# One row-maximum instruction over two PSUM banks instead of two in the layer attention of a hybrid kernel

## The chip, the cores and the metric

The kernel runs on one core of a Trainium2 chip. Its time is the device time of one execution in microseconds; of several executions the median is given. TensorE is called PE here (its weight loads PEld), VectorE DVE, ScalarE ACT, GpSimd POOL, and SyncE, which issues every DMA of this stage, SP.

## What is computed

The program has a stack of four layers, then a feed-forward network with sixteen experts, a second attention, and the experts again. The change touches only the attention inside the four layers. Cut to it, the reference is:

```
# x: 16 sequences of 256 tokens, 128 features; H = 16 heads of 8 features
for l in range(4):
    m = mamba(x, ...)
    x = ln(x + m, g1[l], be1[l])
    qkv = einsum('bsd,od->bso', x, W_qkv[l]) + b_qkv[l]    # -> q, k, v per head
    scores = einsum('bhqd,bhkd->bhqk', q, k) / sqrt(8)
    wts = softmax(scores, axis=-1)                         # 16 x 16 x 256 x 256
    o = einsum('bhqk,bhkd->bhqd', wts, v)
    x = ln(x + o @ W_ao[l].T + b_ao[l], g2[l], be2[l])
    x = x + mlp(x)
```

The softmax takes off each row's maximum before the exponential, so a maximum over 256 keys is needed for each of 16 sequences, 16 heads and 256 queries, in each of four layers.

## The kernel before

**Two passes over the scores.** For each sequence (called a batch, `b`, 0 to 15) the scores are computed twice. The first pass (`row`, line 948) has the queries on the partitions: one head is two matmuls of 128 queries by 256 keys, which fill one PSUM bank of 512 columns. DVE reduces the bank to two maxima per partition (`maxima`, line 1849) into `hmx`. Heads alternate between banks 0 and 1 (`ps[:, o % 2, :]`, `o` is the place in `ORDER`). When all 16 heads of a batch are reduced, DVE makes the negated maxima in two parts (`minus_max`, lines 1857 and 1859), PE transposes them (line 982), ACT copies them to `hmt` (line 1438), and SP sends them by two DMAs (`send_max`, line 571) into two spare rows of the operand `hqk`. In the second pass (`score`, line 960) the keys are on the partitions and the two spare rows take off the maximum inside the matmul, so that ACT can take the exponential straight from PSUM (line 1445). `values` (line 973) multiplies by v.

**The steady loop.** Each batch has eight steps, p0 to p7. In step p PE computes the row scores of two heads of a later batch (heads 8 to 15 of the next batch in p0 to p3, heads 0 to 7 of the one after it in p4 to p7) and, side by side in other rows of its array, the scores of heads 2p and 2p+1 of the current batch. PE's matmuls of a step wait until both maxima of the step before are done:

```
pe.wait_ge(hd_exp, nth(hd_exp, B, p - 2))
if both:
    pe.wait_ge(hd_max, nth(hd_max, B + ahead, o - 1))
```

Beside the scores a step has one more piece of PE work: p0 the v projection (line 941), p2 the q and k projections of the batch three ahead (`project_qk`, lines 935 and 936), p4 the softmax sums (line 989), p7 the output projection (line 995), p1, p3, p5 and p6 `values`, p5 the transposes of the maxima too. DVE has the two maxima of each step, `minus_max` at the end of p3, and one addition in p7 (line 1865).

**What hangs on p2.** From the projections of p2 a chain runs on other engines: ACT adds the bias (line 1425), POOL splits q and k into parts (`hqks`: casts at lines 2136 and 2137, subtractions at lines 2140 and 2141), SP spills them to HBM with four DMAs (line 556), later brings them back in another layout with four more (`scatter`, line 565). SP's queue is in order; in each batch it holds the spill of batch b+3, then `send_max` of batch b+1, then the scatter of batch b+3. The matmuls of p0 of the next batch wait for `send_max` to land (`pe.wait_ge(hd_mx, ...)`).

**Before the loop.** A layer's attention starts with the row scores of batch 0 (16 heads) and of half of batch 1 (8 heads), 12 pairs of heads. Here each head waits only for its own bank: `pe.wait_ge(hd_max, nth(hd_max, l * BATCH + b, o - 2))` at line 953, so that PE fills one bank while DVE reduces the other. Then comes the first `send_max`, behind the third spill and scatter in SP's queue.

**After it.** Batches 13 to 15 have fewer of these parts (no projections and no spill from batch 13 on, no row scores from p4 of batch 14 on).

Of the kernel before, what the change touches and what calls it, by code (L numbers as in the profile page):

```python
# [14 lines left out]
ALU = mybir.AluOpType  # L15
ACT = mybir.ActivationFunctionType
AX = mybir.AxisListType
# [7 lines left out]
LAYERS, STATES, HEADS, DH = 4, 64, 16, 8  # L25
# [9 lines left out]
GROUPS = 4  # L35
# [23 lines left out]
def build_program(nc, x_d, mw_d, xp_d, tw_d, w12_d, gw_d, idx_d, out_d):  # L59
    ctx = ExitStack()  # L60
    with ctx:
# [7 lines left out]
        def at(name, shape, dt=F32, where=None):  # L69

            where = top if where is None else where
            n = 4
            for s in shape[1:]:
                n *= s
            t = nc.alloc_sbuf_tensor_at(name, shape, dt, offset=where[0])
            where[0] += (n + 63) // 64 * 64
            return t
# [129 lines left out]
        hmx = at("hmx", [P, 4, 2, HEADS], where=w)  # L207
# [27 lines left out]
        ps = ctx.enter_context(nc.psum_tensor("ps", [P, 8, CH], F32))  # L235
# [7 lines left out]
        def counter(name, n=1):  # L243

            s = sem(name)
            counted[s.name] = (s, n)
            return s
# [115 lines left out]
        hd_am = counter("hd_am", 16)  # L363
        hd_max = counter("hd_max", 16)
# [32 lines left out]
        def nth(s, c, k=0):  # L397

            n = counted[s.name][1]
            return n * c + (n * CREDIT + k + 1)  # L400

        def every(s, c):

            n = counted[s.name][1]
            return n * c + n * (CREDIT + 1)
# [24 lines left out]
        def scattered(e, third, r):  # L430

            return e * (NR[r] * SPREAD) + third * SPREAD + SPREAD
# [13 lines left out]
        def heads(eng, step, last):  # L446

            step(0, 0, first=True)
            with eng.Fori(0, 3) as i:
                for k in range(4):  # L450
                    step(i * 4 + (1 + k), (1 + k) % 4)
            step(13, 1, n3=False)
            step(14, 2, n2=False, n3=False)
            step(15, 3, n1=False, n2=False, n3=False)
            last()
# [8 lines left out]
        def _(sp):  # L464
# [28 lines left out]
            def attention(e, probsparse):  # L493
                def send_max(b, half, r):

                    B = e * BATCH + b

                    for row, part, ready in ((96, mh, at_mh), (97, ml, at_ml)):
                        sp.wait_ge(ready, nth(ready, B, half))
                        sp.dma_start(qv[r][row:row + 1, 8 * half:8 * half + 8, :].bitcast(F32),  # L500
                                     part[0:8, half, :].bitcast(F32)).then_inc(at_mx[half], 16)

                def spill_qk(b, third, r, first=False):

                    B = e * BATCH + b
                    if not first:
                        before, rb = third + (r + 2) // 3 - 1, (r + 2) % 3
                        sp.wait_ge(at_scat[rb], scattered(e, before, rb))
                    sp.wait_ge(at_lo, nth(at_lo, B, 1))
                    sp.dma_start(qk_d.rearrange("a p t n -> p a t n"), qks[:].bitcast(F32)).then_inc(at_spill, 16)  # L510

                def spread_qk(b, r):


                    B = e * BATCH + b
                    sp.wait_ge(at_spill, every(at_spill, B))
                    sp.wait_ge(at_sc, nth(at_sc, B - 3, 7))
# [1062 lines left out]
        def _(dve):  # L1580
            V = nc.vector
# [261 lines left out]

            def head_attention(l, part="middle"):
                def maxima(b, o, r):
                    B = l * BATCH + b
                    j, g = ORDER[o] // 4, ORDER[o] % 4
                    dve.wait_ge(hd_am, nth(hd_am, B, o))
                    V.tensor_reduce(hmx[:, r, :, 4 * g + j], ps[:, o % 2, :].rearrange("p (t k) -> p t k", t=2), AX.X,  # L1849
                                    ALU.max).then_inc(hd_max, 1)  # L1850

                def minus_max(b, r):

                    B = l * BATCH + b
                    dve.wait_ge(hd_max, nth(hd_max, B, 15))
                    dve.wait_ge(hd_tp, nth(hd_tp, B - 1))
                    V.tensor_scalar(hhl[:, :, 0, :], hmx[:, r], -1.0, None, ALU.mult).then_inc(hd_mhi, 1)
                    dve.wait_ge(hd_mhi, nth(hd_mhi, B))
                    V.scalar_tensor_tensor(hhl[:, :, 1, :], hmx[:, r], -1.0, hhl[:, :, 0, :].bitcast(F32),
                                           ALU.mult, ALU.subtract).then_inc(hd_mlo, 1)  # L1860

                def add_out(b):
                    B = l * BATCH + b
                    dve.wait_ge(hd_aop, nth(hd_aop, B))
                    V.scalar_tensor_tensor(xa[:, ds(b * SEQ, SEQ)], ps[:, 7, 0:SEQ], hbo[:],
                                           xa[:, ds(b * SEQ, SEQ)], ALU.add, ALU.add).then_inc(hd_ao, 1)

                def step(b, r, first=False, n1=True, n2=True, n3=True):
                    for p in range(8):
                        ahead, o, ra = (1, 8 + 2 * p, (r + 1) % 4) if p < 4 else (2, 2 * p - 8, (r + 2) % 4)  # L1870
                        if n1 if p < 4 else n2:
                            maxima(b + ahead, o, ra)
                            maxima(b + ahead, o + 1, ra)
                        if p == 3 and n1:
                            minus_max(b + 1, (r + 1) % 4)
                        if p == 7 and not first:
                            add_out(b - 1)

                if part == "end":
                    return [lambda: add_out(15)]  # L1880

                for o in range(HEADS):
                    maxima(0, o, 0)
                minus_max(0, 0)
                for o in range(8):
                    maxima(1, o, 1)
                heads(dve, step, lambda: None)

            def gates(n):
# [138 lines left out]
            with dve.Fori(0, LAYERS) as l:  # L2028
                dve.wait_ge(load_m, l * 48 + 48)
                dve.sem_inc(waited, 1)  # L2030
                m1(l)
                m2(l)
                m3(l)
                dve.wait_ge(load_f, l * 16 + 16)
                dve.sem_inc(waited, 1)
                dve.wait_ge(load_t, l * 16 + 16)
                dve.sem_inc(waited, 1)
                norm(l * 2 + 1, gain=("g1", "be1"), hooks={"apart": None})
                head_attention(l)
                end = head_attention(l, "end")  # L2040
                norm(l * 2 + 2, gain=("g2", "be2"),
                     hooks={(0, 2): end[0],
                            (1, 0): lambda: f_parts(l, 0), (1, 1): lambda: f_parts(l, 1)})
                f(l)
# [283 lines left out]
```

## Time and profile before

| what | value |
|---|---|
| median of 3 runs | 3271.56 us (3259.83 to 3273.29) |
| profiled execution, own time | 3267.46 us |
| its span, first to last instruction | 3265.8 us |
| mean granted clock of PE | 0.933 |
| busy: PE, DVE, ACT, POOL | 86%, 57%, 54%, 25% |
| maxima (line 1849) | 1024 instructions, 660.1 us busy |

The four layer attentions take about 275 us each of the span. Times in the rows are microseconds from the span's start. A busy share is a mean over stages with different limits, so it says little about one stage; the idle time in front of an instruction, with what ended it, says more.

### The profile page before, as it was taken

How to read it: one execution, taken by the hardware profiler on the slowest of the kernel's cores; microseconds unless marked ns; L12 is line 12 of the kernel's file. 1: busy time of each engine (PE TensorE's matmuls, PEld its weight loads, DVE VectorE, ACT ScalarE, POOL GpSimd, SP SyncE). 2: the span in 40 equal slices, each digit the busy share in tenths (PEclk: the TensorE clock that was granted, in tenths of full speed). 3: DMA queues.
4: the chain of work that ended last, by engine and by line, in shares of the span. 5: the costliest groups of instructions: out<-in, count | busy, mean ns of one | idle time of the engine just before them, and what ended most of it. 6: DMA issues, size and time to landing. Idle time of an engine off the chain costs nothing.

```text
span 3265.8 us, 56810 instructions
## 1 busy us (share of the span) xinstructions
PE 2812.3 (86%) x17396; PEld 1737.5 (53%) x17396; DVE 1863.4 (57%) x3116; ACT 1770.7 (54%) x2669; POOL 805.1 (25%) x864
## 2 busy tenths in 40 slices
PE   7877799787899787898788879999966999799999
PEld 4444446444455444464444446666644777466666
DVE  4567735577546577445677345444536887454444
ACT  6457656367655377654477654444422666544443
POOL 0212200122100222101122014444440000244444
PEclk8989999799899699999799989999987999899999
DMA  2134300244200344101344000000002332000000
GB/s 94 43 94 108 79 6 8 67 100 107 52 12 8 89 103 104 26 8 33 93 99 98 6 7 1 0 0 0 0 1 94 98 101 72 4 4 7 3 6 6
DMA packets 95850, 150.50 MB, mean 46 GB/s; under 512 B 13152, under 2 KB 81248, under 8 KB 89312
## 3 DMA queue, kind: packets, MB, share of 16 engines
q1 hardware_dynamic: 95712, 148.77, 17.3%
q8 instruction: 73, 1.20, 0.2%
q14 instruction: 65, 0.53, 0.1%
HBM read 79.00 MB, written 67.11 MB: 45 GB/s over the span
## 4 chain that ended last, share of the span: by engine, by line
PE 43%; issue 23%; DVE 13%; POOL 11%; DMA 4%; SPq 2%; ACT 2%; DVEq 1%; POOLq 1%; ACTq 0%
POOL hhlo L2179 9%; DVE hmx L1849 9%; PE ps L948 7%; PE ps L754 3%; PE ps L973 2%; PE ps L717 2%; PE ps L681 2%; PE ps L687 2%; PE ps L793 2%; PE ps L829 2%; PE ps L1154 1%; DMA hqk<-hqk_scratch 1%; PE ps L815 1%; SPq L556 1%; DMA hqk_scratch<-hqks 1%
## 5 line engine op out<-in xcount | busy, mean ns | idle before, releaser
L1849 DVE TENSOR_REDUCE hmx<-ps 128x2 f32<-128x512 f32 x1024 | 660.1, 687 | 310.9 <-PE ps L948 310.1
L1445 ACT ACTIVATE hpt<-ps 128x1024 f32<-128x1024 f32 x512 | 522.3, 1024 | 289.5 <-PE ps L960 287.7
L2179 POOL TENSOR_TENSOR hhlo<-hh,hhh 128x512 fp32r<-128x512 f32 x320 | 414.8, 1296 | 463.0 <-ACT hhh L1524 462.1
L948 PE MATMUL ps<-hqk 24*128 24x256 f32 x2048 | 309.0, 359 | 235.1 <-DVE hmx L1849 189.1
L948 PEld LDWEIGHTS ps<-hqk 24*128 24x128 f32 x2048 | 191.5, 206 | 461.8 <-DVE hmx L1849 412.1
L1519 ACT ACTIVATE sil<-ps 128x512 f32<-128x512 f32 x320 | 191.0, 597 | 441.4 <-PE ps L1156 437.4
L1943 DVE TENSOR_TENSOR su<-ps,sil 128x512 f32<-128x512 f32 x256 | 177.1, 692 | 326.7 <-PE ps L1156 318.4
L973 PE MATMUL ps<-hpt,hvx 128*32 128x256 f32 x4096 | 299.3, 413 | 1.9 <-ACT hpt L1445 1.6
L960 PE MATMUL ps<-hqk 26*128 26x256 f32 x2048 | 272.2, 348 | 1.7 <-ACT hpt L1445 1.2
L1524 ACT ACTIVATE hhh<-hh 128x512 fp32r<-128x512 f32 x320 | 199.5, 624 | 40.9 <-DVE hh L1946 26.8
L2136 POOL CAST hqks<-hqk 128x512 fp32r<-128x512 f32 x64 | 40.5, 633 | 673.3 <-ACT hqk L1425 641.8
L1946 DVE TENSOR_TENSOR hh<-ps,su 128x512 f32<-128x512 f32 x256 | 177.0, 691 | 8.7
L960 PEld LDWEIGHTS ps<-hqk 26*128 26x128 f32 x2048 | 162.7, 197 | 25.5 <-ACT hpt L1445 19.7
L1757 DVE TENSOR_REDUCE mxs<-ps 128x2 f32<-128x512 f32 x256 | 164.1, 680 | 12.9 <-PE ps L793 11.7
L1373 ACT ACTIVATE pt<-ps 128x1024 f32<-128x1024 f32 x128 | 130.3, 1019 | 66.1 <-PE ps L815 64.3
L973 PEld LDWEIGHTS ps<-hpt,hvx 128*32 128x32 f32 x4096 | 113.0, 115 | 94.0 <-issue 22.9
L1154 PE MATMUL ps<-xh,w2h 128*128 128x512 f32 x324 | 154.7, 477 | 0.0
L2148 POOL TENSOR_TENSOR hon<-hraw,hrec 128x512 f32<-128x512 f32 x64 | 81.6, 1275 | 270.4 <-ACT hrec L1459 270.4
L1350 ACT ACTIVATE hid<-ps,mw 128x512 f32<-128x512 f32 x128 | 83.1, 689 | 106.3 <-PE ps L746 105.2
L1154 PE MATMUL ps<-xh,w1h 128*128 128x512 f32 x324 | 128.2, 396 | 13.1 <-DVE hh L1940 9.6
L1167 PE MATMUL ps<-hhh,w3h 128*128 128x512 f32 x320 | 127.3, 398 | 4.4 <-POOL hhlo L2179 4.4
L1155 PE MATMUL ps<-xl,w1h 128*128 128x512 f32 x324 | 128.8, 397 | 0.0
(247 smaller groups left out, 5593.1 us busy)
## 6 DMA issues: line engine op xcount, KB each, us to landing
hqk_scratch<-hqks SPq DMA_DIRECT2D x256, 192.0 KB, 3.1
hqk<-hqk_scratch SPq DMA_DIRECT2D x256, 192.0 KB
qk_scratch<-qks SPq DMA_DIRECT2D x16, 768.0 KB, 3.3
k<-qk_scratch SPq DMA_DIRECT2D x16, 384.0 KB
qv<-qk_scratch SPq DMA_DIRECT2D x64, 96.0 KB
mw<-mw_in SPq DMA_DIRECT2D x10, 516.5 KB, 3.9
w12raw<-w_in SPq DMA_DIRECT2D x1, 2560.0 KB, 9.5
streams<-x_in SPq DMA_DIRECT2D x8, 256.0 KB, 4.8
```

What stands on the lines that cost most here:

```text
L948: return mm(ps[:, o % 2, qt * SEQ:(qt + 1) * SEQ], hqk[r][32 * g:32 * g + 24, 0, j, qt * P:(qt + 1) * P], hqk[r][32 * g:32 * g + 24, 1, j, ...
L960: return mm(ps[:, 2 + g, kt * SEQ:(kt + 1) * SEQ], hqk[r][32 * g:32 * g + 26, 1, j, kt * P:(kt + 1) * P], hqk[r][32 * g:32 * g + 26, 0, j, ...
L973: last = mm(ps[32 * g:32 * g + 32, 6, (j // 2) * SEQ:(j // 2 + 1) * SEQ], hvx[r][:, kt, g, j, :], hpt[:, j, g, kt, :], start=j % 2 + kt == ...
L1154: mm(o, wh[:, k, :], xh[:, u, :], start=True, stop=False)
L1445: A(hpt[:, j, g:g + 2, :, :], ps[:, 2 + g:4 + g, :], ACT.Exp, scale=QSCALE).then_inc(hd_exp, 1)
L1519: A(sil[:, k % 2, :], ps[:, k % 2, :], ACT.Silu).then_inc(e_s, 1)
L1524: A(hhh[:, b % 4, :], hh[:, b % 2, :], ACT.Copy).then_inc(e_hi, 1)
L1757: V.tensor_reduce(mxs[:, r, h, :], ps[:, h % 2, :].rearrange("p (t k) -> p t k", t=2), AX.X, ALU.max)\
L1849: V.tensor_reduce(hmx[:, r, :, 4 * g + j], ps[:, o % 2, :].rearrange("p (t k) -> p t k", t=2), AX.X, ALU.max).then_inc(hd_max, 1)
L1943: V.tensor_tensor(su[:, s, :], ps[:, 2 + s, :], sil[:, s, :], ALU.mult).then_inc(e_t, 1)
L1946: V.tensor_tensor(hh[:, s, :], ps[:, 4 + s, :], su[:, s, :], ALU.mult).then_inc(e_m, 1)
L2179: G_.tensor_tensor(hhlo[:, k % 4, :], hh[:, k % 2, :], hhh[:, k % 4, :].bitcast(F32), ALU.subtract).then_inc(e_lo, 1)
```

## The change

In the layer attention one instruction now reduces both banks, two heads at a time, where there were two instructions of one bank each. Its output is four maxima per partition, for two heads and two halves of the queries; it waits for the row scores of both heads and then counts `hd_max` up by two. The diff:

```
             def head_attention(l, part="middle"):
                 def maxima(b, o, r):
+
                     B = l * BATCH + b
                     j, g = ORDER[o] // 4, ORDER[o] % 4
-                    dve.wait_ge(hd_am, nth(hd_am, B, o))
-                    V.tensor_reduce(hmx[:, r, :, 4 * g + j], ps[:, o % 2, :].rearrange("p (t k) -> p t k", t=2), AX.X,
-                                    ALU.max).then_inc(hd_max, 1)
+                    dve.wait_ge(hd_am, nth(hd_am, B, o + 1))
+                    V.tensor_reduce(hmx[:, r].rearrange("p t (g j) -> p g j t", g=GROUPS)[:, g:g + 2, j, :],
+                                    ps[:, 0:2, :].rearrange("p u (t k) -> p u t k", t=2), AX.X, ALU.max)\
+                     .then_inc(hd_max, 2)
...
                         if n1 if p < 4 else n2:
                             maxima(b + ahead, o, ra)
-                            maxima(b + ahead, o + 1, ra)
...
-                for o in range(HEADS):
+                for o in range(0, HEADS, 2):
                     maxima(0, o, 0)
                 minus_max(0, 0)
-                for o in range(8):
+                for o in range(0, 8, 2):
                     maxima(1, o, 1)
                 heads(dve, step, lambda: None)
```

The program of PE, with its waits, is the same in both kernels, and so are those of ACT, POOL and SP. DVE's changes. In the loop, at the end of p3, its rows before were (`hd_am` counts finished row scores, `hd_tp` the transposes, `hd_mhi` the first part of the negated maxima):

```order
L1848 REGISTER_ALU
L1849 TENSOR_REDUCE hmx<-ps 128x2 [waits hd_am]
L1848 REGISTER_ALU
L1849 TENSOR_REDUCE hmx<-ps 128x2 [waits hd_am]
L1848 REGISTER_ALU
L1849 TENSOR_REDUCE hmx<-ps 128x2 [waits hd_am]
L1856 REGISTER_ALU [waits hd_max]
L1857 TENSOR_SCALAR hhl<-hmx 128x2x16 [waits hd_tp]
L1858 REGISTER_ALU
L1859 SCALAR_TENSOR_TENSOR hhl<-hmx,hhl 128x2x16 [waits hd_mhi]
L1848 ISA
L1849 TENSOR_REDUCE hmx<-ps 128x2 [waits hd_am]
```

and at the same place of the changed kernel (its line numbers are one or two higher):

```order
L1849 REGISTER_ALU
L1850 TENSOR_REDUCE hmx<-ps 128x2x2 [waits hd_am]
L1849 REGISTER_ALU
L1850 TENSOR_REDUCE hmx<-ps 128x2x2 [waits hd_am]
L1858 REGISTER_ALU [waits hd_max]
L1859 TENSOR_SCALAR hhl<-hmx 128x2x16 [waits hd_tp]
L1860 REGISTER_ALU
L1861 SCALAR_TENSOR_TENSOR hhl<-hmx,hhl 128x2x16 [waits hd_mhi]
L1849 ISA
L1850 TENSOR_REDUCE hmx<-ps 128x2x2 [waits hd_am]
```

Two reduces of 128x2 outputs became one of 128x2x2; what follows them kept its order. Before the loop, PE's rows are these in both kernels, from the first head on (`hd_scat`: the operand has landed):

```order
L953 ISA [waits hd_scat]
L948 MATMUL ps<-hqk_133 128x256 [waits hd_max]
L948 MATMUL ps<-hqk_133 128x256
L953 REGISTER_ALU
L948 MATMUL ps<-hqk_133 128x256 [waits hd_max]
L948 MATMUL ps<-hqk_133 128x256
L953 REGISTER_ALU
L948 MATMUL ps<-hqk_133 128x256 [waits hd_max]
```

The wait of each head is for the head two before it. Nothing moved here, but `hd_max` now reaches the counts that two neighbouring heads wait for at the same moment.

## Rows read from the trace of the kernel before

**Rows 1.** The page's costliest groups: busy, mean ns, idle before, releaser

```profile
L1849 DVE TENSOR_REDUCE hmx<-ps 128x2 f32<-128x512 f32 x1024 | 660.1, 687 | 310.9 <-PE ps L948 310.1
```

**Rows 2.** Timeline, batch 8, p1 and p2: start, length, instruction, idle before

```profile
307.39 0.38 PE L948 MATMUL ps<-hqk 24*128 24x256 f32 x2 [0.70 <-DVE hmx L1849]
...
307.93 1.29 DVE L1849 TENSOR_REDUCE hmx<-ps 128x2 f32<-128x512 f32 x2 [0.59 <-PE ps L948]
...
309.27 0.39 PE L948 MATMUL ps<-hqk 24*128 24x256 f32 x2 [0.38 <-DVE hmx L1849]
```

**Rows 3.** One line, a long DVE instruction: duration min/median/max in ns

```profile
L2023 DVE TENSOR_TENSOR w1l<-w12raw,w1h x1: 2825/2825/2825, 30.9 to 30.9; 128x2560 fp32r<-128x2560 f32 x1
```

**Rows 4.** Timeline, layer 0, batch 8, end of p3 to the next p0

```profile
312.61 0.62 POOL L2137 CAST hqks<-hqk 128x512 fp32r<-128x512 f32 x1
...
313.10 0.18 DVE L1857 TENSOR_SCALAR hhl<-hmx 128x32 fp32r<-128x32 f32 x1
...
313.31 0.72 POOL L2140 TENSOR_TENSOR hqks<-hqk,hqks 128x256 fp32r<-128x256 f32 x1
313.32 0.76 DVE L1859 SCALAR_TENSOR_TENSOR hhl<-hmx,hhl 128x32 fp32r<-128x32 f32 x1
...
320.97 0.38 PE L948 MATMUL ps<-hqk 24*128 24x256 f32 x2 [0.31 <-DVE hmx L1849]
```

**Rows 5.** One line, all executions of the second part of minus_max

```profile
L1859 DVE SCALAR_TENSOR_TENSOR hhl<-hmx,hhl x64: 191/474/766, 168.3 to 1806.5; 128x32 fp32r<-128x32 f32 x64
```

**Rows 6.** Timeline, layer 1, from the end of p3 to the next p0

```profile
747.24 0.38 PE L948 MATMUL ps<-hqk 24*128 24x256 f32 x2 [0.31 <-DVE hmx L1849]
...
749.40 0.19 DVE L1859 SCALAR_TENSOR_TENSOR hhl<-hmx,hhl 128x32 fp32r<-128x32 f32 x1
...
749.65 1.29 DVE L1849 TENSOR_REDUCE hmx<-ps 128x2 f32<-128x512 f32 x2
...
750.99 2.57 SPq L556 DMA_DIRECT2D hqk_scratch<-hqks  x4
...
756.80 0.38 PE L948 MATMUL ps<-hqk 24*128 24x256 f32 x2 [0.48 <-DVE hmx L1849]
```

**Rows 7.** The p2 projection by layer, window from batch 1 on: first and last start

```profile
L935 PEld LDWEIGHTS ps<-streams,tw x24: 186/189/333, 201.2 to 371.7; 128*128 128x128 f32 x24
...
L935 PEld LDWEIGHTS ps<-streams,tw x24: 186/189/333, 667.1 to 838.1; 128*128 128x128 f32 x24
...
L935 PEld LDWEIGHTS ps<-streams,tw x24: 186/189/333, 1131.3 to 1304.3; 128*128 128x128 f32 x24
...
L935 PEld LDWEIGHTS ps<-streams,tw x24: 186/189/333, 1595.9 to 1769.5; 128*128 128x128 f32 x24
```

**Rows 8.** Timeline, layer 0, before the loop

```profile
161.14 0.79 PE L948 MATMUL ps<-hqk 24*128 24x256 f32 x4
...
161.97 1.29 DVE L1849 TENSOR_REDUCE hmx<-ps 128x2 f32<-128x512 f32 x2 [0.96 <-PE ps L948]
...
163.54 1.29 DVE L1849 TENSOR_REDUCE hmx<-ps 128x2 f32<-128x512 f32 x2 [0.28 <-PE ps L948]
...
173.27 1.29 DVE L1849 TENSOR_REDUCE hmx<-ps 128x2 f32<-128x512 f32 x2 [0.28 <-PE ps L948]
...
179.41 0.58 PE L948 MATMUL ps<-hqk 24*128 24x256 f32 x2 [5.58 <-DMA hqk<-hmt]
```

**Rows 9.** What the row-score matmuls waited for: us in total, times

```profile
DMA hqk<-hmt: 26.1, 10
```

**Rows 10.** Timeline, PE at p0 in layers 1 and 3

```profile
710.68 0.38 PE L948 MATMUL ps<-hqk 24*128 24x256 f32 x2 [0.99 <-DMA hqk<-hmt]
...
1640.51 0.38 PE L948 MATMUL ps<-hqk 24*128 24x256 f32 x2 [0.74 <-DMA hqk<-hmt]
```

**Rows 11.** Windows: busy time by engine (x instructions), then PE's granted clock

```profile
1161.30:1164.80 3.50, 3.50 (x31) 1.89 (x28) 2.18 (x4) 2.36 (x3) 0.00 (x0) 0.51 0.48 105
...
1642.60:1649.50 6.90, 6.90 (x56) 3.46 (x56) 3.72 (x6) 4.40 (x6) 0.69 (x2) 0.51 0.43 101
```

## The prediction

> **What bounds the kernel now.** I read the costliest groups first: the maxima are DVE's largest item, 1024 instructions of 687 ns, and DVE stood idle in front of them for 310.9 us until PE's row scores were there [rows 1]. So the two engines wait for each other, and the timeline of one step shows how: PE's matmuls begin at 307.39, DVE begins its pair 0.54 later, is busy for 1.29, and PE begins the next step 0.05 after the pair's end [rows 2]. The sum, 1.88 us, is the step (307.39 to 309.27). PE had stood idle for 0.38 us before it, so in a step with `values` PE has 0.38 us to spare: a DVE that is faster by less than that shows in full.
>
> Two steps of a batch are special. At the end of p3 `minus_max` stands between two maxima. Its second part takes 0.76 us in layer 0, from 313.32 to 314.08, beside POOL's subtraction of line 2140 from 313.31 to 314.03 [rows 4]; in the batch of [rows 6] it takes 0.19. Over all 64 the shortest is 191 ns, the longest 766, and the median 474 lies between the two sorts, so half of them are long [rows 5]. The long sort holds up the next maxima to about 1.0 us after PE's start, where 0.53 is usual (749.12 to 749.65 [rows 6]): about 0.45 us a batch. The other special step is p0, which waits for `send_max`. A batch with the long sort lasts 11.70 us from p2 to the next p0 (309.27 [rows 2] to 320.97 [rows 4]) and two steps more, 15.46. With the short sort p2 stands one step before 747.24, at 745.36, and the next p0 at 756.80 [rows 6]: 11.44, and 15.20 for the batch. Only 0.26 of the 0.45 is kept, because the spill issues until 753.56, `send_max` stands behind it on SP, and p0 comes 3.24 after that.
>
> **The change part by part.**
>
> *The merged maximum.* Not in the trace. The lower price is from DVE's slope: 512 columns take 687 ns [rows 1], 2560 take 2825 [rows 3], so 1.044 ns a column, and 1024 columns take 687 + 512 x 1.044 = 1222 ns. The upper bound is two separate instructions, 2 x 687 = 1374 ns. I take 1.22, since the long instruction is of the same engine and type. Against the pair's 1.29 that saves 0.07. The wait for the second head costs little in the loop: PE issues both heads side by side, within one row of the timeline [rows 2]; I give it 0.01. A step gains 0.06 (bounds: 0.07 gained, 0.09 lost).
>
> *minus_max against POOL.* POOL's chain starts from the projections of p2, DVE's `minus_max` comes after two more maxima, so it moves ahead of POOL by 2 x 0.06 = 0.12 us. Now it arrives at 313.32, 0.01 after line 2140 has begun [rows 4]. With 0.12 less it comes before it. The cast of line 2137 ends at 313.23, in the changed kernel about 0.37 after the maxima's end; the first part would run beside it, the second just behind it. I take the short sort in all batches. The Trainium skill, SBUF — State Buffer, section Who interferes with whom, says that a DVE instruction with two SBUF inputs, or one in a two-port mode, contends with POOL and that whoever issues first keeps the port for its whole instruction; the second part agrees (0.76 against 0.19 [rows 4, 6]). By that rule the first part would also wait for the cast's end, where its row shows 0.18 us beside the cast [rows 4]; the next maxima would come some 0.04 later, under 2 us in all, and that lies behind the wait of the next item.
>
> *send_max.* With eight steps of 1.82 DVE and PE alone would need some 14.6 a batch. But from p2 on the chain projections, ACT, POOL, spill, `send_max` does not shorten: p0 stays 11.44 after p2 [rows 6]. Only p0 and p1 gain: 11.44 + 2 x 1.82 = 15.08, and I add 0.05 for landings that are later in some batches (the waits of [rows 10]). So 15.13, and PE waits about 0.45 at each p0 on top of its 0.25 now.
>
> *Sum for the loop.* From p2 of batch 1 to p2 of batch 12 are 11 batches: 170.5, 171.0, 173.0 and 173.6 us [rows 7], together 688.1. At 15.13 they are 665.7. The surplus now over 15.46 is 7.9; I keep 5 of it for the first batches of each layer, which run at half clock: 670.7, a gain of 17.4. One more batch a layer gains 1.3. Some 12 other steps a layer, of batches 0, 13 and 14, gain 0.06 each where DVE bounds them, say 2.5 in all.
>
> *Before the loop.* Here the change takes an overlap away. Before, PE fills one bank while DVE reduces the other, and a pair comes every 1.57 (161.97 to 163.54 [rows 8]). Now both banks free at once: PE needs 0.83 until DVE can start (161.14 to 161.97), DVE 1.22, the handover 0.05: 2.11. Eight of the eleven intervals grow by 0.54, two by about 0.4 (PE's rows already lay partly beside `minus_max` and the transposes), and the one with the bias matmuls shrinks by 0.14, together 5.0 us. The last maxima end at 174.56 and would end at 179.5; p0 starts at 179.41 on the landing of `send_max` [rows 8]. The cover is 4.8 us wide, so 0.1 sticks out in this layer, and up to 0.8 in a layer where the DMA is earlier. `send_max` itself has some 3.5 us of room behind the scatter and loses 3.1. I take 1.3 us lost for four layers; without the cover it would be 20.
>
> *PE's clock.* In the loop PE had short stretches at a granted clock of 0.51, that is 1.2 GHz in place of 2.4 [rows 11]. Each came right after a p0 that waited for `send_max`: 0.74 idle at 1640.51 and half clock from 1642.60; but 0.99 idle at 710.68 [rows 10] was followed by none. Of ten such waits [rows 9] four are those before the loops; of the six in it three were followed by half clock. The shorter waits, as in [rows 6], were not. In 6.90 us at half clock DVE did 6 instructions [rows 11], where a batch has 19 in 15.46, so 8.5: 2.0 us lost, 1.0 for a stretch of 3.5, and more where the projections of p2 fall into it, since POOL's chain is late then. Layer 2, with two such stretches, takes 2.0 more than layer 1 with none [rows 7]. I price one at 1.5. In the changed kernel every p0 has about 0.7 idle before it. I take 12 stretches in 44 batches, a little over one in four: 18 us lost.
>
> Sum: -17.4 - 1.3 - 2.5 + 1.3 + 18 = -1.9 us against the profiled execution's 3267.46, so 3265.6. That execution is 4.1 under the median of 3271.56 and inside the runs' spread. I predict 3266.
>
> **The rivals.**
>
> *A. The clock holds* (0.25). A step is shorter, so PE is denser outside p0, and 0.99 idle did not bring the clock down once [rows 10]. With three stretches the sum is -20 + 4.5 = -15: 3252. Against it: three of six.
>
> *B. send_max does not bind* (0.03), if SP took it before the spill or it landed a good half microsecond sooner: 14.6 a batch, about 48 less: 3219. Against it stands SP's order of issue.
>
> *C. The clock falls after most p0* (0.12): a wait on a DMA in each batch, and half clock behind it. It decides from 14 stretches on, where the gain of 20 turns into a loss; with 28 it is -20 + 42 = +22: 3289, with all 48 +52: 3319. For it: all p0 now wait as the three did. Against: the wait of 710.68. The Trainium skill, TensorE: Matmul & The Clock Gate, section HAM oscillation — how this bites in real kernels, tells of a kernel in which a wait for a DMA at each tile brought the clock down at every single tile; its waits were several times longer than ours, and by it the time would be the 3319.
>
> *D. The merged maximum costs as two* (0.05): 1.37, so a step is 0.09 longer, 400 steps: +36, less with POOL's collision as now: 3303.
>
> *The forecast*, most of the gain given back (0.55): 3256 to 3280.
>
> **How the numbers follow.** A difference under 0.5% (16 us) can't be told from none here. Faster by more means under 3255: rival B and nearly all of A, with the fringe of the forecast, 0.29. Slower by more means over 3288: D and most of C, with a fringe, 0.16. The rest is 0.55. The range of 8 in 10 leaves out B, the far half of C and D and the edge of A: 3246 to 3287. It takes in the price of the step (0.05 to 0.07 gained, some 2 us) and the count of stretches, 3 to 22.
>
> **What would show it.** The maxima: 512 instructions of about 1222 ns. `minus_max`'s second part: 191 to 200 ns in all 64. Full-clock steps of 1.82. p0's matmuls waiting for the DMA of `hmt` in some 40 batches, with 0.7 idle. A batch of 15.1 at full clock. Pairs of 2.11 before the loop, and p0 of batch 0 hardly later. Half-clock stretches in the loops: about 12; their number moves the result most, and makes it wrong if it is far from that. The prediction is wrong in its core if a merged maximum takes over 1.3 us or POOL's collision stays.

## The result and the profile after

| | before | after |
|---|---|---|
| median | 3266.86 us, 4 runs (3259.83 to 3273.29) | 3291.42 us, 4 runs (3289.86 to 3296.87) |
| profiled execution, own time | 3267.46 | 3296.87 |
| its span | 3265.8 | 3295.2 |
| maxima: count and mean | 1024 of 687 ns | 512 of 1225 ns |

The ratio on record, which is not the quotient of the two medians (1.0075), is 1.0082, 95% interval 1.0062 to 1.0102: slower by 0.8%, where 3266 was predicted and the range ended at 3287. The two spans differ by 29.4 us; 25.3 of them lie in the four layer attentions, each taken from the start of its first maximum to the start of its last.

The page's costliest groups for the maxima (columns as in [rows 1]):

```profile
L1850 DVE TENSOR_REDUCE hmx<-ps 128x4 f32<-128x1024 f32 x512 | 627.1, 1225 | 368.9 <-PE ps L948 367.8
```

DVE is busy 33 us less (660.1 in [rows 1]), and idle in front of the maxima 58 us more (310.9 there). The instruction got cheaper and the wait ahead of it dearer. A step of a normal batch shows how. The timeline of the changed kernel, batch 7 of layer 0, p0 and p1 (columns as in [rows 2]):

```profile
297.07 0.38 PE L948 MATMUL ps<-hqk 24*128 24x256 f32 x2 [0.35 <-DVE hmx L1850]
...
297.71 1.23 DVE L1850 TENSOR_REDUCE hmx<-ps 128x4 f32<-128x1024 f32 x1 [0.30 <-PE ps L948]
...
298.99 0.38 PE L948 MATMUL ps<-hqk 24*128 24x256 f32 x2 [0.73 <-DVE hmx L1850]
```

PE starts at 297.07 and DVE at 297.71, 0.64 later; in [rows 2] it was 0.54. The maximum takes 1.23 in place of the pair's 1.29, and the handover is 0.05 in both. The step is 1.92 (297.07 to 298.99) where it was 1.88. So the saving of 0.06 is there, but the start is 0.10 later, and that is more.

The records of DVE below the level of that view tell where 0.07 of the 0.10 is. Start in us, length in ns, line, instruction; `>=` is a wait on a semaphore, `++` counts one up, `+=` more than one. The changed kernel:

```
299.563    21  L1849  EVENT_SEMAPHORE  $S[220]>=
299.628  1225  L1850  TENSOR_REDUCE    hmx<-ps  $S[221]+=
```

The kernel before:

```
307.927   694  L1849  TENSOR_REDUCE    hmx<-ps  $S[220]>=  $S[221]++
308.535   683  L1849  TENSOR_REDUCE    hmx<-ps  $S[220]>=  $S[221]++
```

Before, one instruction waits, reduces and counts one up. After, `then_inc(hd_max, 2)` made the count a `+=`, and the wait stands in an instruction of its own, 0.065 us ahead of the reduce (64 to 71 ns in the 477 places where it stands right in front of one). The other 0.03 is the second head's mark: in the semaphore's own record the two marks of `hd_am` lie 34 ns apart in both kernels (299.501 and 299.535 here), and the merged maximum waits for the second.

The same timeline at the end of p3, as [rows 4]:

```profile
303.46 1.23 DVE L1850 TENSOR_REDUCE hmx<-ps 128x4 f32<-128x1024 f32 x1 [0.69 <-PE ps L948]
304.25 0.61 POOL L2138 CAST hqks<-hqk 128x512 fp32r<-128x512 f32 x1
...
304.81 0.18 DVE L1859 TENSOR_SCALAR hhl<-hmx 128x32 fp32r<-128x32 f32 x1
304.94 0.72 POOL L2141 TENSOR_TENSOR hqks<-hqk,hqks 128x256 fp32r<-128x256 f32 x1
...
305.03 0.69 DVE L1861 SCALAR_TENSOR_TENSOR hhl<-hmx,hhl 128x32 fp32r<-128x32 f32 x1
...
305.64 1.21 DVE L1850 TENSOR_REDUCE hmx<-ps 128x4 f32<-128x1024 f32 x1
```

and that line over the whole run, as [rows 5]:

```profile
L1861 DVE SCALAR_TENSOR_TENSOR hhl<-hmx,hhl x64: 191/680/690, 172.3 to 1833.0; 128x32 fp32r<-128x32 f32 x64
```

The collision with POOL stays. The second part of `minus_max` starts 0.78 after the cast (304.25 to 305.03), where it was 0.71 in [rows 4]: two longer steps have moved it back by 0.07, not ahead. It is long, over 600 ns, in 37 of 64 (32 before). The next maximum starts 0.95 after the end of the last (304.69 to 305.64) where a step has 0.69: 0.26 lost. So a batch is 8 x 1.92 + 0.26 = 15.62; the median of batches 2 to 12 is 15.60, against 15.46 before. Hardly anything waits for `send_max` any more, as what the row-score matmuls waited for shows (us in total, times; [rows 9] had 26.1, 10 for the second of these):

```profile
  DVE hmx L1850: 723.3, 908
...
  DMA hqk<-hmt: 1.5, 2
```

Before the loop, as [rows 8]:

```profile
160.71 0.88 PE L948 MATMUL ps<-hqk 24*128 24x256 f32 x4 [1.39 <-DVE hmx L1850]
...
161.70 1.23 DVE L1850 TENSOR_REDUCE hmx<-ps 128x4 f32<-128x1024 f32 x1 [1.04 <-PE ps L948]
162.98 0.88 PE L948 MATMUL ps<-hqk 24*128 24x256 f32 x4 [0.45 <-DVE hmx L1850]
...
181.07 0.58 PE L948 MATMUL ps<-hqk 24*128 24x256 f32 x2 [1.39 <-DVE hmx L1850]
```

A pair comes every 2.26 (161.70 to 163.96), with 0.99 from PE to DVE. p0 now starts at 181.07 on the maxima, no longer on the DMA at 179.41. Over four layers the stretch from the first maximum to that of the first p0 is 8.2 us longer.

### The profile page after: what moved, and what is told of

Its sections match the earlier page's. It is cut to its first block, busy times and chain, and to the rows that moved or that the text cites. A ratio compares the mean times of both kernels' runs of the same rounds, so it can differ in the third digit from the quotient of the medians.

```text
span 3295.2 us, 56298 instructions
## 1 busy us (share of the span) xinstructions
PE 2806.8 (85%) x17396; PEld 1727.6 (52%) x17396; DVE 1830.3 (56%) x2604; ACT 1767.7 (54%) x2669; POOL 802.2 (24%) x864
## 4 chain that ended last, share of the span: by engine, by line
PE 46%; DVE 20%; issue 18%; POOL 10%; DMA 2%; ACT 2%; SPq 1%; DVEq 1%; POOLq 1%; ACTq 0%
DVE hmx L1850 17%; POOL hhlo L2180 9%; PE ps L948 9%; PE ps L754 3%; PE ps L973 3%; PE ps L717 2%; PE ps L681 2%; PE ps L687 2%; PE ps L793 2%; PE ps L829 2%; PE ps L1154 1%; PE ps L815 1%; PE ps L632 1%; PE ps L1155 1%; PE ps L1156 1%
## 5 line engine op out<-in xcount | busy, mean ns | idle before, releaser
L1850 DVE TENSOR_REDUCE hmx<-ps 128x4 f32<-128x1024 f32 x512 | 627.1, 1225 | 368.9 <-PE ps L948 367.8
L948 PE MATMUL ps<-hqk 24*128 24x256 f32 x2048 | 293.0, 363 | 268.4 <-DVE hmx L1850 246.1
L948 PEld LDWEIGHTS ps<-hqk 24*128 24x128 f32 x2048 | 178.1, 209 | 496.6 <-DVE hmx L1850 477.2
```

Source lines behind the costliest of these rows:

```text
L948: return mm(ps[:, o % 2, qt * SEQ:(qt + 1) * SEQ], hqk[r][32 * g:32 * g + 24, 0, j, qt * P:(qt + 1) * P], hqk[r][32 * g:32 * g + 24, 1, j, ...
L1850: V.tensor_reduce(hmx[:, r].rearrange("p t (g j) -> p g j t", g=GROUPS)[:, g:g + 2, j, :], ps[:, 0:2, :].rearrange("p u (t k) -> p u t k", ...
```

## The experiments

In each run the kernel before ran on the same chip; its median was 3262.32 (e1 to e4), 3261.51 (e5, e6, e7, e9) and 3263.89 (e8, e10 to e12). The table sums up the traces, one of each kernel; its last two columns come from all runs, and the ratio is again the one on record, not the quotient of the medians. "Start" is from PE's first matmul of a step to DVE's maximum, "step" from one maximum to the next (both the median of 464 steps); "long" counts the second part of `minus_max` above 600 ns, of 64; "batch" is the median of batches 2 to 12 at p0; "p0 late" is the median time from the end of the last maximum to PE's p0, less the usual 0.055; "falls" are stretches at a granted clock of about 0.5, the 1.2 GHz level, that start in batches 2 to 12 of the four layers.

| kernel | start | step | long | batch | p0 late | falls | median us | ratio to before, interval |
|---|---|---|---|---|---|---|---|---|
| before | 0.536 | 1.881 | 32 | 15.46 | 0.00 | 3 | 3262 | |
| after | 0.639 | 1.920 | 37 | 15.60 | 0.00 | 7 | 3291.42 | 1.0082, 1.0062 to 1.0102 |
| e1 pairs counted | 0.569 | 1.850 | 0 | 15.13 | 0.33 | 13 | 3270.42 | 1.0018, 1.0001 to 1.0035 |
| e2 one mark | 0.612 | 1.893 | 42 | 15.47 | 0.00 | 2 | 3275.58 | 1.0034, 1.0013 to 1.0054 |
| e3 both | 0.543 | 1.825 | 0 | 15.07 | 0.45 | 12 | 3267.29 | 1.0012, 0.9992 to 1.0032 |
| e4 old start | 0.639 | 1.920 | 38 | 15.60 | 0.00 | 6 | 3291.44 | 1.0087, 1.0058 to 1.0116 |
| e5 before, late wait | 0.570 | 1.917 | 37 | 15.64 | 0.00 | 7 | 3286.74 | 1.0071, 1.0048 to 1.0095 |
| e6 before, merged start | 0.538 | 1.883 | 43 | 15.47 | 0.00 | 1 | 3275.78 | 1.0044, 1.0027 to 1.0060 |
| e7 e3, old start | 0.545 | 1.826 | 0 | 15.09 | 0.44 | 14 | 3262.55 | 0.9998, 0.9978 to 1.0018 |
| e8 e12, split spill | 0.543 | 1.825 | 0 | 15.28 | 0.11 | 3 | 3259.75 | 0.9992, 0.9977 to 1.0008 |
| e9 e3, p7 filled | 0.545 | 1.825 | 0 | 15.07 | 0.45 | 0 | 3244.27 | 0.9948, 0.9928 to 0.9968 |
| e10 before, p7 filled | 0.535 | 1.881 | 32 | 15.61 | 0.05 | 1 | 3260.12 | 0.9985, 0.9971 to 1.0000 |
| e11 after, p7 filled | 0.638 | 1.919 | 44 | 15.61 | 0.01 | 0 | 3291.81 | 1.0090, 1.0071 to 1.0109 |
| e12 e7, p7 filled | 0.543 | 1.825 | 0 | 15.06 | 0.45 | 0 | 3243.40 | 0.9940, 0.9921 to 0.9960 |

### e1 to e3: which part of the late start is which

e1 takes the changed kernel and counts pairs, so that the maximum counts up by one again:

```
-        hd_max = counter("hd_max", 16)
+        hd_max = counter("hd_max", 8)
...
-                     .then_inc(hd_max, 2)
+                     .then_inc(hd_max, 1)
```

with the waits on `hd_max` in PE and `minus_max` divided by two. e2 keeps the count of two and gives PE one mark for each pair:

```
-                                    if t == 1:
+                                    if t == 1 and u == 1:
                                         last.then_inc(hd_am, 1)
```

with `hd_am` a counter of 8. e3 has both.

> One edit to the changed kernel: hd_max counts pairs of heads, so that the merged maximum adds 1 and not 2. Theory S (the signals): with an addition of 2 the maximum can't carry its own wait, and a wait instruction of its own stands ahead of it, which costs 0.07 us a step. Then DVE starts 0.57 us after PE in place of 0.64, a step is 1.85, minus_max gets ahead of POOL's subtraction (0.19 us, not 0.69), p0 is then bound by send_max at about 15.15 a batch, and the time falls by 10 to 20 us, to 3271 to 3281, the width being PE's half-clock stretches. Theory B (the two banks): an instruction that reads two banks starts later whatever signals it has; the start stays at 0.64 and the time at 3291 within 3.

> One edit to the changed kernel: PE marks the row scores of a pair once, with the second head's last matmul, and hd_am counts pairs. Theory S: the second of two marks that are due at the same moment arrives 0.034 us after the first; with one mark DVE starts 0.60 to 0.61 after PE in place of 0.64 and a step is 1.89. minus_max stays behind POOL's subtraction. The time falls by 3 to 8 us, to 3283 to 3288. Theory B: nothing moves (3291 within 3, start at 0.64).

> Both edits: one mark a pair and hd_max counted in pairs, so that the merged maximum has its wait and its signal on itself. Theory S: DVE starts 0.54 after PE as in the kernel before, a step is 1.82, minus_max's second part 0.19 in all batches, a full-clock batch 15.08 to 15.15 bound by send_max at p0, and the time is what the prediction's sum said with the measured start before the loop, 3262 to 3280: 3262 if PE's clock holds in the loop, 3280 if it falls in a third of the batches. Theory B: 3291 within 3.

Measured: the start is 0.070 earlier in e1, 0.027 in e2 and 0.096 in e3, so the two parts add up. With both gone the start is that of before, so reading two banks adds nothing to it (theory B is out). A step of e3 in its timeline:

```profile
297.11 0.38 PE L948 MATMUL ps<-hqk 24*128 24x256 f32 x2 [0.67 <-DVE hmx L1852]
...
297.65 1.23 DVE L1852 TENSOR_REDUCE hmx<-ps 128x4 f32<-128x1024 f32 x1 [0.60 <-PE ps L948]
...
298.93 0.38 PE L948 MATMUL ps<-hqk 24*128 24x256 f32 x2 [0.32 <-DVE hmx L1852]
...
742.17 0.39 PE L948 MATMUL ps<-hqk 24*128 24x256 f32 x2 [0.71 <-DMA hqk<-hmt]
...
743.99 0.53 PE L948 MATMUL ps<-hqk 24*128 24x256 f32 x2 [0.67 <-DVE hmx L1852]
```

The step is 1.82. In layer 1 the p0 of 742.17 waits with 0.71 idle for the DMA, and p1 has its usual 0.67 right behind it ([rows 2] had 0.70 there). The second part of `minus_max`, and what the row scores waited for, in e3:

```profile
L1863 DVE SCALAR_TENSOR_TENSOR hhl<-hmx,hhl x64: 191/192/193, 171.6 to 1795.8; 128x32 fp32r<-128x32 f32 x64
```

```profile
  DVE hmx L1852: 634.8, 848
  DMA hqk<-hmt: 37.0, 49
```

Before the loop, e3's maxima and its first p0:

```profile
161.50 1.23 DVE L1852 TENSOR_REDUCE hmx<-ps 128x4 f32<-128x1024 f32 x1 [0.90 <-PE ps L948]
...
179.78 0.58 PE L948 MATMUL ps<-hqk 24*128 24x256 f32 x2 [1.33 <-DVE hmx L1852]
```

The second part of `minus_max` is short in all 64, and the row scores wait for the transfer of the maxima 49 times. So e3 is the kernel that the prediction described: steps of 1.82, no collision, batches of 15.07 bound by `send_max`, 12 falls of the clock, 3267 us. The removed late start is worth 24 us (3291.4 to 3267.3). e1 alone gets 21 of them: its step of 1.850 is already short enough to end the collision. e2, whose step is not, gets 16, where 3 to 8 were expected. In its trace batches 2 to 12 are 8.1 us shorter than in the changed kernel, about what the shorter step makes; another 10.9 lie in the rest of the attentions, and why they moved was not followed. The terms do not add up in time as they do in a step: whether DVE or POOL comes first at `minus_max` is all or nothing, and the falls of the clock go their own way.

Single traces differ in such parts without any order: batch 0, over the four layers, takes between 65.3 us (e8) and 76.8 (e11), and everything outside the attentions between 2245.0 and 2255.3. A difference of a few microseconds between two traces therefore settles little by itself.

### e5: the late wait without the merged instruction

The kernel before, single maxima, with the first of each pair in the loop waiting for the second head's mark:

```
-                    dve.wait_ge(hd_am, nth(hd_am, B, o))
+                    dve.wait_ge(hd_am, nth(hd_am, B, o if own else o | 1))
```

(`own` is set before the loop, where nothing changes.)

> The kernel before, with its two maxima a step, but in the loop the first of them waits for the row scores of both heads. Theory S: the second head's mark is 0.034 us later, so a step is 1.915, nearly that of the changed kernel (1.92), with nothing merged; minus_max moves 0.07 back against POOL and stays behind its subtraction. If the length of the step is the cause of the loop's loss, this loses in the loop what the changed kernel does, 6 us for 44 batches and up to 10 with half-clock stretches: 3272 to 3280 where the kernel before has 3262. Theory B (reading two banks in one instruction is the cause): no loss, 3262 within 4.

One step in its timeline:

```profile
297.68 0.39 PE L948 MATMUL ps<-hqk 24*128 24x256 f32 x2 [0.41 <-DVE hmx L1849]
...
298.25 1.29 DVE L1849 TENSOR_REDUCE hmx<-ps 128x2 f32<-128x512 f32 x2 [0.63 <-PE ps L948]
...
299.59 0.38 PE L948 MATMUL ps<-hqk 24*128 24x256 f32 x2 [0.35 <-DVE hmx L1849]
```

The start is 34 ns later and the step 0.036 longer, for 25 us in the median (3286.74 against 3261.51). Steps alone would make 0.036 x 464 = 17. The instruction and its work are those of before, so a wait of 34 ns in every step is by itself enough for most of a loss of the size that the change had. It cost more than the 10 to 18 us that I had put down for it. In the trace the attentions are 16.0 us longer than before's, what the steps alone make; where the other 9 of the median come from is open.

### e4, e6, e7: the pairs before the loop

e4 is the changed kernel with single maxima before the loop, e7 the same for e3 (with counters of their own for that part), e6 the kernel before with merged maxima there only. e4's edit, whose mirror image is e6's:

```
-                for o in range(0, HEADS, 2):
-                    maxima(0, o, 0)
+                for o in range(HEADS):
+                    maximum(0, o, 0)
```

> The changed kernel, but before the loop each head has its own maximum again, as in the kernel before; the loop keeps the merged one with its late start. If the lost overlap before the loop is what it looks like in the trace, pairs take 1.57 there again in place of 2.26, the first p0 comes 25.3 us after the first maximum in place of 27.1, the four layers gain 8 us, and up to 4 more if PE's half-clock stretch at the start gets shorter: 3279 to 3284. If the cover of the DMA hides it, as the prediction had it, under 2 us: 3290.

> The other part of the change alone: the kernel before in the loop, the merged maximum only before it, in each layer. If the lost overlap reaches the end, pairs take 2.26 there, the first p0 is 2 us later in each layer, and the time rises by 8 us over the kernel before, 3270 where that has 3262. If the DMA of the maxima covers it, the time is the same within 3.

> The kernel with both signals mended (e3_both) and, before the loop, one maximum a head again with counters of their own, so that PE and DVE overlap there as in the kernel before. A step of 1.825, no collision with POOL, pairs of 1.57 before the loop. If parts add: e3_both's time less 7 us (its start before the loop is 7.3 us longer over four layers), 3260, level with or 2 us under the kernel before; the half-clock stretches of the loop, some 12, stay.

e6 costs 14 us in the median and 11.1 in the trace of the attentions: 7.8 before the loop and 4.3 in batch 0, the batches after that as before. So merging there costs, in this kernel. Taking it back does not always give that: e4's stretch before the loop is only 1.1 longer than before's in place of 8.2, but batch 0 is 2.7 us and batches 2 to 12 are 2.7 longer than in the changed kernel, and the median is the same. e7 is 4.7 under e3 by the medians, with intervals that overlap, and in its trace the attentions are 4.5 longer than e3's. So only the cost of merging before the loop is shown (e6); that taking it back helps the other kernels is not.

### e9 to e12: PE kept busy ahead of p0

e9 is e3 with one more matmul of 256 columns in p7, which the two after it write over:

```
                 def out(b):
                     pe.wait_ge(hd_on, nth(hd_on, l * BATCH + b))
+                    mm(ps[:, 7, 0:SEQ], T("wo", 0, D), hon[:, 0, :], start=True, stop=True)
```

e10, e11 and e12 put the same line into the kernel before, the changed kernel and e7.

> e3_both with one more 256-column matmul in p7 (its result is overwritten by the one that follows), which takes 0.4 us of the 0.7 us in which PE waits before p0. If the half-clock stretches in the loop come from that idle time, they go from 12 to under 4 and the time falls by about 1.5 us for each, 10 to 15 in all: 3253 to 3257. If they come from something else the time is that of e3_both, 3267 within 4; if p7 has become the bound, slower by 0.2 a batch, 9 us.

> The kernel before with one more matmul of 256 columns at the start of every p7 (written over by the two that follow), nothing else. It tells how much of the gain of the filled version (3244 against 3261.5 in its call) is the filling and how much the merged maximum. Theory (the filling only keeps the TensorE clock up; in the kernel before only 3 stretches at half clock start inside the loop, 13.6 us): those 3 cost about 1.2 to 1.6 us each, so 4 us less, about 3258 with before at 3262, batch 15.46 as before. Rival 1 (the extra matmul costs its own 0.2 us a batch on the path): 60 x 0.2 = 12 us more, 3274. Rival 2 (the filling gives the whole gain in any version): about 3244.

> The changed kernel with the same extra matmul in p7. Theory (its loss is the 0.1 us later start of every maximum, 1.92 us a step, the clock only a small part): the 7 stretches at half clock inside the loop (23.8 us) go, 7 times about 0.8 us for a batch of 16.4 instead of 15.6, so about 6 us less, 3285, with the batch still at 15.60. Rival (the loss is mainly the clock): the time falls to that of before, 3262.

> Merged maximum with a counter of pairs and one mark, single maxima before the loop, and the extra matmul in p7. From its parts: the filled version with merged maxima before the loop ran 3244 (before 3261.5); single maxima there took 4.7 us off in the unfilled version (3262.6 against 3267.3 in two calls), and the pairs before the loop are 2 us a layer longer when merged. Theory: 3244 - 5 to 8 = 3236 to 3240, no stretch at half clock inside the loop, batch 15.07. Rival (what the start gives is lost again in the first batch of the loop, as in the version with the old start of the changed kernel, 3291.4 against 3291.4): 3244.

Batches 2 to 12 of layer 1 in e3 and, in the first fall there, what a stretch at half clock looks like (columns: window, its length, busy us and instructions of PE, PEld, DVE, ACT, POOL, then the granted clock, the share of the DMA engines and GB/s):

```profile
682.20:854.20 172.00, 142.85 (x1585) 74.33 (x1586) 118.55 (x122) 123.15 (x165) 46.67 (x66) 0.94 0.42 103
744.20:750.90 6.70, 6.70 (x56) 3.47 (x60) 3.24 (x3) 4.08 (x6) 0.34 (x1) 0.50 0.32 68
```

The same batches of e9, with as many instructions of DVE:

```profile
668.50:834.40 165.90, 139.59 (x1606) 74.34 (x1606) 118.34 (x122) 123.14 (x165) 46.67 (x66) 1.00 0.44 107
```

The clock is 1.00 throughout and the 11 batches are 6.1 us shorter. The end of p7 and the p0 after it in e9:

```profile
314.55 0.70 PE L996 MATMUL ps<-hon,tw 128*128 128x256 f32 x2
...
315.09 1.03 PE L998 MATMUL ps<-hon,tw 128*128 128x256 f32 x4
...
316.38 0.39 PE L948 MATMUL ps<-hqk 24*128 24x256 f32 x2 [0.27 <-DMA hqk<-hmt]
```

PE's idle time ahead of p0 is 0.27 in place of 0.71, so only p1's is left of the two; p0 itself is as late as in e3 (0.45 behind the maxima), so the wait for `send_max` did not change and the clock did. Over the four layers batches 2 to 12 are 15.1 us shorter than in e3, which had 12 falls: 1.26 us for each. The median fell by more, 23 us, where 10 to 15 were expected; 6.2 us of it lie in the other batches of the traces. The filled e3 is the first version that beats both kernels, by 0.5%. e12 is level with it by the medians, where its theory had 3236 to 3240. Its attentions are 8.4 us shorter than e9's in the traces, but its span only 2.4: the other 6.0 are within what the parts outside the attentions vary by. So it is not shown whether the old start gives anything here.

In the kernel before, whose p0 is not bound by the DMA, the filling alone gains nothing clear of noise (0.9985, 0.9971 to 1.0000), and it has a price. PE in e10, from the last matmuls of a p7 to the next p0:

```profile
304.83 1.03 PE L996 MATMUL ps<-hon,tw 128*128 128x256 f32 x4
305.91 0.39 PE L948 MATMUL ps<-hqk 24*128 24x256 f32 x2
```

PE goes on 0.05 after the filled p7's end, where it had 0.31 of idle time ([rows 4], 320.97). So p0 is late by 0.05, its maxima start 0.63 after PE instead of 0.53, and a batch takes 15.61 where it took 15.46: the first rival of e10's expectation. In the changed kernel the filling removes all 7 falls, and the time stays, 3291.81: I had expected 6 us less. In its trace batches 2 to 12 are 2.5 us shorter and batch 0, which has no extra matmul, is 4.0 longer. So those 7 falls were a small part of the loss at most.

### e8: the transfer of the maxima ahead of the fourth spill

e12 with SP issuing the three first transfers of the spill, then `send_max`, then the fourth:

```
-                        spill(b + 3)
+                        spill(b + 3, (0, 1, 2))
                     if n1:
                         send_max(b + 1, (r + 1) % 4)
+                    if n3:
+                        spill(b + 3, (3,))
```

> As the kernel with single maxima before the loop and the filling, and SyncE issues the two transfers of the next batch's maxima ahead of the fourth transfer of the spill instead of behind it. In the filled version the fourth spill transfer takes SyncE 0.62 us just ahead of them (312.55), they are issued at 313.21, and PE waits 0.45 us for them in p0 of nearly every batch, 15.07 us a batch. Theory (the transfer of the maxima is what bounds the batch): it lands about 0.6 us earlier, p0 waits for the maxima alone, 8 x 1.825 = 14.60 us a batch; 48 batches x 0.45 = 21 us less than the version without the split, about 3217. Rival 1 (minus_max itself, not SyncE, is late: when the batch is shorter it comes too late for the earlier place): 15.07 stays, no change. Rival 2 (the fourth spill, now later, makes the scatter late and p4 waits for it): p4 waits 0.6 us instead, no change.

3259.75 us (0.9992, 0.9977 to 1.0008): 16 us slower than e12. SP's issues in its timeline, and PE at the following p4:

```profile
297.90 1.91 SPq L562 DMA_DIRECT2D hqk_scratch<-hqks  x3
300.77 1.23 SPq L577 DMA_DIRECT2D hqk<-hmt  x2
302.10 0.62 SPq L562 DMA_DIRECT2D hqk_scratch<-hqks  x1
304.90 1.52 SPq L571 DMA_DIRECT2D hqk<-hqk_scratch  x4
...
311.95 0.38 PE L955 MATMUL ps<-hqk 24*128 24x256 f32 x2 [0.91 <-DMA hqk<-hqk_scratch]
```

p0 is late by 0.11 in the median instead of 0.45, so `send_max` was what bound it. But SP sat from 299.81 to 300.77 until the maxima were ready, with the fourth spill transfer behind that wait; the scatter went out late and p4 waits for it, 0.49 in the median. This is the second rival of its expectation: the wait moved from p0 to p4, and batches are 15.28. That rival had no change of the time. Instead it is 16 us; of the 15.8 us by which the attentions are longer in the traces 13.9 lie in batches 2 to 12, which had 3 falls, and why they cost so much is open.

## Why the prediction was wrong

**The step that failed** is the price of a later start in "a step gains 0.06". The prediction has one term for it: "The wait for the second head costs little in the loop ...; I give it 0.01." That wait measured 0.03 (e2, e5). The count of two had no term at all, and it measured 0.07, for a wait that has become an instruction (e1). Together the start is 0.103 later. I read the two heads as simultaneous because the timeline puts them into one row; 34 ns do not show there. And I took the diff's count of two for free, without a reason. The Trainium skill, Trainium Kernel Development and Optimization, section Key Constraints, says that compute semaphores increment by 1. The trace shows a count of two carried out, and the 0.065 us that it cost. The step went to 1.92 in place of 1.82. A loss of 0.04 a step lies inside the bounds that I had kept (0.07 gained, 0.09 lost), but on the other side of zero from the value taken, and everything behind it hung on that sign. By the prediction's own test, "wrong in its core if ... POOL's collision stays", it is wrong in its core, though not for the reason that stands there.

**The maximum itself** was right: 1226 ns for 1222. Rival D (1.37) is out.

**minus_max against POOL** was right as a mechanism and went the other way with the longer step. e1 and e3 show it: steps shorter by 0.03 or 0.06, short in all 64. The lead is smaller than I had worked out, 0.01 us instead of 0.11. In e3's timeline:

```profile
302.27 0.62 POOL L2140 CAST hqks<-hqk 128x512 fp32r<-128x512 f32 x1
...
302.65 0.28 DVE L1861 TENSOR_SCALAR hhl<-hmx 128x32 fp32r<-128x32 f32 x1
...
302.96 0.19 DVE L1863 SCALAR_TENSOR_TENSOR hhl<-hmx,hhl 128x32 fp32r<-128x32 f32 x1
302.97 0.77 POOL L2143 TENSOR_TENSOR hqks<-hqk,hqks 128x256 fp32r<-128x256 f32 x1
```

The first part ends at 302.93, 0.04 behind the cast's end at 302.89, and the second starts 0.01 ahead of the subtraction. By the rule that the prediction gave from the Trainium skill, SBUF — State Buffer, section Who interferes with whom, the first part waits for the cast's end as well; the trace agrees, in all 52 batches in which POOL has this work. The 0.18 us of [rows 4] did not speak against it: that one, too, ended 0.05 after the cast (313.28 and 313.23).

**send_max** was never reached in the changed kernel (2 waits, 1.5 us). In e3 it bound as forecast: 15.07 for the 15.08 that the chain gave (my allowance of 0.05 was not needed), p0 late by 0.45. e8 confirms it from the other side.

**The loop's gain** of 17.4 us for 11 batches a layer is what e9 shows once the clock holds: batches 2 to 12 are 18.3 us shorter than before's, which had 3 falls.

**The start.** Pairs of 2.11 were forecast; they are 2.12 in e3 (161.50 to 163.62) and 2.26 with the two late parts. The cover of the DMA was 4.8 us wide and, as worked out, just used up: e3 loses 1.8 us over four layers (1.3 forecast). With 2.26 the maxima stick out, 8.2. Here the mis-sized step did its second damage.

**The clock.** Twelve falls at 1.5 us, 18 in all, were forecast for short steps; e3 has 12 at 1.26, 15 in all. e9 shows that they end when PE's idle time ahead of p0 is filled. In the changed kernel itself there were 7, and six of them came in a batch whose p0 had waited for the maxima, 0.35 to 0.52 us, and not for the DMA; in e5 it was again six of seven. So a wait for `send_max`, to which the prediction tied the falls, is not needed for one. Rival C, a fall at nearly each p0, did not come: 12 of 44 batches with the same wait of 0.7. The page TensorE: Matmul & The Clock Gate, section HAM oscillation — how this bites in real kernels, of the Trainium skill tells of a fall at every tile behind longer waits; no batch 2 to 12 of these kernels has waits that long at p0, so that is not tried here; waits of 0.7 us brought falls in about one batch of four.

**The sum.** e3's spans stand at -5.3 against before's profiled one, where the prediction had -1.9, and its median is within 0.2% of before. Nearly the whole miss of 25 us is then the late start: 24.1 between e3 and the changed kernel. That e3's 3267 lies so near to the 3266 is partly luck: the sum started from 3267.46, and the kernel before had a median of 3262 beside e3, so e3 did not gain. In the attentions of the two traces (28.7 us apart) it is 13.4 in batches 2 to 12, 6.4 before the loop, and 9.0 in batches 0, 1, 13 and 14. The 4.1 us by which the spans of before and after differ outside the attentions are within what these parts vary by among the fourteen traces (10.3).

## What to carry to other kernels

When two instructions are merged, look at the synchronisation as closely as at the work: which mark the merged one now waits for, and whether its count is still one. Count pairs instead of adding two, and mark once per pair. Where two engines wait for each other in every step, a few hundredths of a microsecond are the whole stake: with 34 ns more in each of 464 steps this kernel was 25 us slower (e5), 17 of them from the steps themselves.

What a shorter step gives can be taken back by the clock. A single extra matmul in front of the wait of p0 made the difference between no gain (e3) and 0.5% (e9). Neither part shows a gain alone, and where PE has no wait to fill, the extra matmul lengthens the batch (e10).

## What the runs showed of the hardware

- A DVE instruction that waits and counts one up is a single record; with a count of two the wait is an instruction of its own, and the start 0.065 to 0.07 us later (e1 against after).
- Marks of two matmul groups issued side by side came 34 ns apart; waiting for the later one delays DVE by 27 to 34 ns.
- A reduce of 1024 columns in PSUM across two banks takes 1225 ns, two of 512 together 1.29 us: against the 1222 ns that the slope of single instructions gives, crossing the bank costs nothing that shows.
- DVE's `tensor_scalar` on 32 columns, 0.18 us alone, took 0.22 to 0.60 beside a POOL cast (e1, e3), ending 0.03 to 0.04 after it in every batch. DVE's next instruction was then 0.01 ahead of POOL's in all 52 batches with POOL's work, which makes the order stable.
- In e3, where PE was idle for 0.7 us at p0 and again at p1, the 1.2 GHz level followed in 12 of 44 batches; in e9, with 0.28 at p0 in the median and 0.6 at p1, in none. In the kernel before most batches had 0.31 at p0 and 0.7 at p1, and its 3 falls stood behind a p0 that waited for the DMA. The changed kernel, with 0.35 and 0.73, had 7.
